# Layer 0's self attention in a two-layer decoder: the output projection written to another PSUM bank, the residual's moments taken later

## The reference

```python
x = _layernorm(x + _L0_attn_ref(x, Wg, bg, Wv, bv, Wo, bo))
g = x @ Wg.T + bg;  v = x @ Wv.T + bv            # then split into heads
dot = einsum('bhid,bhjd->bhij', g, g)
corr = dot / (nrm[..., :, None] * nrm[..., None, :] + 1e-08)
corr = (corr * m + 1.0) / 2.0                    # m: causal mask
denom = mean(corr, axis=3) + 0.5
sum_inv = sum(1.0 / denom, axis=2, keepdims=True)    # over the rows
weighted = corr * (1.0 / (denom * sum_inv))[..., None]
attn = softmax(weighted * m + (1.0 - m) * NEG)
out = einsum('bhij,bhjd->bhid', attn, v)  ->  out @ Wo.T + bo
```

## Time and profile before

| | us |
|---|---|
| median of 3 runs | 2441.64 |
| lowest, highest run | 2436.2, 2446.11 |
| profiled execution, own time | 2436.9 |
| its span in the trace | 2435.0 |
| PE busy | 2222.8 (91%) |
| DVE busy | 1337.9 (55%) |
| ACT busy | 1107.0 (45%) |
| POOL busy | 917.7 (38%) |

### The profile page before, as it was taken

The page is one execution under the profiler, slowest core; times in us unless marked ns, Lnnn a source line. Parts: engine busy times, 40 slices in busy tenths (PEclk is TensorE's granted clock), DMA queues, the critical chain, the costliest instruction groups (busy, mean ns, idle before and its releaser), DMA issues. The chain is left out here.

```text
span 2435.0 us, 44061 instructions
## 1 busy us (share of the span) xinstructions
PE 2222.8 (91%) x16870; PEld 1746.6 (72%) x16870; DVE 1337.9 (55%) x2486; ACT 1107.0 (45%) x1904; POOL 917.7 (38%) x935
## 2 busy tenths in 40 slices
PE   6888886899997999999999799999995999999993
PEld 5777775566665666757777588888884888888893
DVE  6888886688885870024555468888784111111113
ACT  3677775456655664434333355555552111111113
POOL 4777774244444680000110234544453122222221
PEclk8999998899999999999999899999997999999997
DMA  4444553101011679460220323333332766566665
GB/s 144 112 113 116 159 138 90 57 18 53 28 62 43 237 253 301 144 217 5 66 70 27 122 79 103 107 105 105 107 120 103 272 185 196 180 176 189 191 203 149
DMA packets 204607, 313.05 MB, mean 129 GB/s; under 512 B 63601, under 2 KB 183153, under 8 KB 191089
## 3 DMA queue, kind: packets, MB, share of 16 engines
q1 hardware_dynamic: 184336, 255.12, 33.2%
q0 software_dynamic: 13440, 17.90, 4.1%
q10 hardware_dynamic: 6624, 37.23, 3.9%
HBM read 188.75 MB, written 121.45 MB: 127 GB/s over the span
## 5 line engine op out<-in xcount | busy, mean ns | idle before, releaser
L2758 ACT ACTIVATE dec_area<-me_ps_h 128x512 f32<-128x512 f32 (+1 forms) x160 | 88.7, 555 | 423.5 <-PE me_ps_h L2736 414.8
L2799 DVE TENSOR_SCALAR me_yo<-me_ps_y,moe_xg 128x256 f32<-128x256 f32 x72 | 34.8, 484 | 429.6 <-PE me_ps_y L2746 410.6
L2674 POOL DMA_INDIRECT xo<-me_yo,me_row x72 | 112.8, 1566 | 410.4 <-DVE me_yo L2799 347.1
L2209 POOL TENSOR_TENSOR l1x_e<-l1x_e,l1x_ri 128x1024 f32<-128x1024 f32 x64 | 121.8, 1903 | 240.3 <-DVE l1x_ri L2469 240.3
L2736 PE MATMUL me_ps_h<-me_xt,me_w 128*128 128x256 f32 (+1 forms) x1056 | 210.0, 357 | 0.0
L2746 PE MATMUL me_ps_y<-me_w,dec_area 128*128 128x256 f32 x944 | 209.2, 379 | 0.7 <-DVE me_yo L2799 0.7
L2746 PEld LDWEIGHTS me_ps_y<-me_w,dec_area 128*128 128x128 f32 x944 | 178.7, 190 | 25.1 <-issue 1.1
L2736 PEld LDWEIGHTS me_ps_h<-me_xt,me_w 128*128 128x128 f32 x1056 | 181.7, 190 | 20.2
L892 POOL TENSOR_TENSOR l0x_e<-l0x_e,l0x_ri 128x1024 f32<-128x1024 f32 x64 | 120.1, 1897 | 187.8 <-DVE l0x_ri L1112 187.8
L2308 PE MATMUL l1x_ps_p<-l1x_xct,dec_area 128*128 128x256 f32 x512 | 126.1, 392 | 0.8 <-ACT l1x_xct L2394 0.7
L2346 PE MATMUL l1x_ps_o<-dec_area,l1x_ot 128*128 128x256 f32 x512 | 120.4, 389 | 1.4 <-ACT l1x_ot L2417 1.4
(11 more groups left out here) (414 smaller groups left out, 5334.8 us busy)
## 6 DMA issues: line engine op xcount, KB each, us to landing
me_w<-in_w SPq DMA_DIRECT2D x33, 2048.0 KB, 9.5
xs<-dec_zero SPq DMA_DIRECT2D x31, 1032.0 KB, 6.9
k<-kv_kt ACTq DMA_DIRECT2D x16, 1024.0 KB, 4.6
v<-kv_va ACTq DMA_DIRECT2D x16, 1024.0 KB, 4.7
l1x_kt<-k SPq DMA_DIRECT2D x16, 1024.0 KB, 5.1
l1x_va<-v SPq DMA_DIRECT2D x16, 1024.0 KB
moe_w_first<-in_w SPq DMA_DIRECT2D x7, 2048.0 KB, 9.5
moe_xg<-xs SPq DMA_DIRECT2D x32, 258.0 KB, 2.9
```

What stands on the lines that cost most here:

```text
L2209: pool.tensor_tensor(e[:, n % 2, u, :, :], e[:, n % 2, u, :, :], spread(ri[:, n % 2, u, :], P), ALU.mult).then_inc(e_scaled, 1)
L2674: pool.indirect_dma_start(token_rows, bass.IndirectOffsetOnAxis(row[:, j % 2, q:q + 1], 0), yo[:, j % 2, q, :], None, compute_op=ALU.add). ...
L2758: act.activation(h[:, j % 2, 2 * i:2 * i + 2, 0:P * size(j)], ps_h[i % HB][:, :, 0:P * size(j)], ACT.Gelu).then_inc(gelued, 1)
```

## The change

The output projection of a tile is written to `ps_a[0]`, in columns 16 to 79 of each of its four parts of 128, instead of 256 adjacent columns of `ps_e[1]`. `residual` reads it there. The transposes of set j = 1 no longer wait for `residual_done`, nor the projection for the copies `et_copied`. Instead `sum_inverse` of tile n waits for the residual of tile n-2, and the denominators of tile n wait for the projection of tile n-2. On VectorE the two moment operations leave `residual` and become a step of their own, behind the even weighting of the next round. On TensorE the second set of transposes is placed ahead of the value projection, and the third ahead of the sum of inverses. ScalarE copies the value projection between the second and the third set instead of behind all four.

```diff
@@ -571,6 +571,9 @@
 
                     return ps_a[0][:, i, 0:H]
 
+                def parts(a):
+                    return a.rearrange("p (a b) -> p a b", a=4)
+
                 def correlate(n, u):
                     i = 2 * n + u
                     item_done(dve, tanh_done, i)
@@ -591,6 +594,8 @@
                     item_done(dve, rows_summed, n)
                     if n + 1 < TILES:
                         dve.wait_ge(ops_copied, 2 * (n + 1) + 1)
+                    if n >= 2:
+                        item_done(dve, multiplied, n - 2)
                     dve.tensor_scalar(small(1), flat(st[:, n % 2, 0, :, :]), 0.25 / S, 1.0, ALU.mult, ALU.add).then_inc(denom_done, 1)
                     item_done(dve, denom_done, n)
                     slot_free(dve, inv_summed, n, 2)
@@ -619,15 +624,18 @@
                     item_done(dve, multiplied, n)
                     item_done(dve, x_biased, n)
                     slot_free(dve, normed, n, 2 * G)
-                    dve.tensor_tensor(r[:, g % 2, t, :], ps_e[1][:, 0:2, :].rearrange("p a b -> p (a b)"), xb[:, n % 2, :],
+                    dve.tensor_tensor(parts(r[:, g % 2, t, :]), ps_a[0][:, :, H:H + D // 4], parts(xb[:, n % 2, :]),
                                       ALU.add).then_inc(residual_done, 1)
+
+                def moments(n):
+                    g, t = n // G, n % G
                     item_done(dve, residual_done, n)
                     slot_free(dve, mv_done, n, 2)
                     dve.bn_stats(stats[:, n % 2, :], r[:, g % 2, t, :]).then_inc(stats_done, 1)
                     item_done(dve, stats_done, n)
                     slot_free(dve, ln_done, g, 2)
                     dve.bn_aggr(mv[:, g % 2, t, :], stats[:, n % 2, :]).then_inc(mv_done, 1)
-                walk([(1, weigh_even), (0, lambda n: fold_bias() if n == 0 else None), (0, lambda n: correlate(n, 1)), (2, divide), (0, row_sums), (2, residual), (-1, lambda n: correlate(n, 0)), (0, fitness)])
+                walk([(1, weigh_even), (0, lambda n: fold_bias() if n == 0 else None), (3, moments), (0, lambda n: correlate(n, 1)), (2, divide), (0, row_sums), (2, residual), (-1, lambda n: correlate(n, 0)), (0, fitness)])
 
             @block.tensor
             def _(pe):
@@ -681,6 +689,8 @@
 
                 def sum_inverse(n):
                     item_done(pe, inv_done, n)
+                    if n >= 2:
+                        item_done(pe, residual_done, n - 2)
                     if n + 1 < TILES:
                         pe.wait_ge(ops_copied, 2 * (n + 1) + 1)
                     pe.matmul(ps_a[0][:, 0, 0:H], ones[:, :], flat(st[:, n % 2, 1, :, :]), start=True, stop=True).then_inc(inv_summed, 1)
@@ -692,8 +702,6 @@
                         slot_free(pe, divided, n, 1)
                     elif j == 1 and n == 0:
                         pe.wait_ge(bo_done, 1)
-                    elif j == 1:
-                        slot_free(pe, residual_done, n, 1)
                     else:
                         pe.wait_ge(et_copied, i - 1)
                     for h in range(4):
@@ -724,12 +732,11 @@
                     if n == 0:
                         pe.wait_ge(w_loaded, 64)
                     item_done(pe, divided, n)
-                    item_done(pe, et_copied, n, 4)
                     for k in range(2):
-                        last = pe.matmul(ps_e[1][:, 0:2, :].rearrange("p a b -> p (a b)"), ot[:, n % 2, k, :], w_o[:, k, :],
+                        last = pe.matmul(ps_a[0][:, :, H:H + D // 4], ot[:, n % 2, k, :], w_o[:, k, :].rearrange("p (a b) -> p a b", a=4),
                                          start=k == 0, stop=k == 1)
                     last.then_inc(multiplied, 1)
-                walk([(3, multiply), (2, lambda n: transpose_e(n, 0)), (0, project_v), (2, lambda n: transpose_e(n, 1)), (1, sum_inverse), (2, lambda n: transpose_e(n, 2)), (2, lambda n: transpose_e(n, 3)), (0, lambda n: score(n, 1)), (2, apply), (-1, transposes), (-1, lambda n: score(n, 0))])
+                walk([(3, multiply), (2, lambda n: transpose_e(n, 0)), (2, lambda n: transpose_e(n, 1)), (0, project_v), (2, lambda n: transpose_e(n, 2)), (1, sum_inverse), (2, lambda n: transpose_e(n, 3)), (0, lambda n: score(n, 1)), (2, apply), (-1, transposes), (-1, lambda n: score(n, 0))])
 
             @block.scalar
             def _(act):
@@ -766,9 +773,9 @@
                     slot_free(act, e_transposed, i, 4, 2)
                     act.activation(e[:, n % 2, u, :, :], wt[:, u, :, :], ACT.Exp).then_inc(exped, 1)
 
-                def copy_et(n):
+                def copy_et(n, which):
                     slot_free(act, applied, n, 1)
-                    for j in range(4):
+                    for j in which:
                         item_done(act, e_transposed, 4 * n + j)
                         act.activation(et[:, j // 2, 4 * (j % 2):4 * (j % 2) + 4, :], ps_e[j % 2][:, :, :], ACT.Copy).then_inc(et_copied, 1)
 
@@ -778,7 +785,7 @@
                     slot_free(act, stored[t], g, 1, 16)
                     act.activation(y[:, t, :], r[:, g % 2, t, :], ACT.Identity, scale=lnm[:, g % 2, 0, t:t + 1],
                                    bias=lnm[:, g % 2, 1, t:t + 1]).then_inc(normed, 1)
-                walk([(8, normalise), (2, lambda n: exponentials(n, 1)), (0, lambda n: guard(n, 0)), (2, copy_et), (0, copy_v), (0, lambda n: guard(n, 1)), (1, lambda n: exponentials(n, 0)), (-1, copy_ops)])
+                walk([(8, normalise), (2, lambda n: exponentials(n, 1)), (0, lambda n: guard(n, 0)), (2, lambda n: copy_et(n, (0, 1))), (0, copy_v), (2, lambda n: copy_et(n, (2, 3))), (0, lambda n: guard(n, 1)), (1, lambda n: exponentials(n, 0)), (-1, copy_ops)])
         kit.clear_semaphores()
 
 
```

## The result

The changed kernel takes 2417.95 us, the median of four runs (2411.71 to 2419.68), beside 2440.53 for the kernel before (2436.2 to 2446.11). The ratio is 0.9901 with a 95% interval of 0.9889 to 0.9913: 22.6 us less, where 24.9 was forecast. The time is 1.2 us above the forecast one, closer than the gain is, because the forecast started from 2441.6 and the kernel before came out at 2440.53 with one more run. The profiled execution took 2417.48 us.

What follows compares the result with a forecast made beforehand. The prediction took a 10.73 us chain of dependent steps across engines, with neither VectorE nor TensorE full, to bound the head loop. Saving 0.86 in 29 rounds gave 2441.6 - 24.9 = 2416.7 us, range 2408 to 2433.

Steps and rivals of the forecast that it cites:

- The ring: Layer 0 self-attention head loop: chain of dependent steps across engines that sets one round, forecast from 10.73 to 9.87 us.
- the two rings: Scores wait for transposes held by the residual, and for the even correlation; removing only the first wait buys 0.19 us.
- The independent pair: VectorE: even correlation does not need the residual's result, so starts 0.08 us before its recorded end, at 234.50.
- TensorE in time: TensorE's reordered work before the scores ends at 235.50, against their release at 235.83: 0.33 us to spare.
- The added waits: Sum of inverses waiting for residual, denominator for projection: cost nothing, at most 0.03 us a round (1 us).
- The short pieces: Projection in four 64-column pieces: forecast free; rival 0.80 us more a tile, gain only 11.3 us, 2430, chance 0.09.
- Where the moments go: VectorE, behind the even weighting: moments fit before the odd correlation with 0.26 us to spare.
- The rival of slower moments: Moments double to 1.12 us beside GpSimd's multiplication; gain 0.56 a round, 16.2 us, 2425; chance 0.11.
- The sum: Whole loop: 29 rounds times 0.86 us gives 24.9 us less.
- The rival of starved issue: TensorE starved of instructions: ten stalls of 3.80 us cost 38 against 24.9 gained, 2455; chance 0.06.
- Prologue and tail: Stretches where one tile alone runs through the engines: forecast no change.

Runs made afterwards that it cites:

- the two halves: Changed kernel with moments left directly behind the residual: 2432.25 us, 0.9962 of before; kernel before with only the moments moved: 2437.18 us, 0.999 of before.
- the old order: Changed kernel with TensorE's and ScalarE's orders put back as in the kernel before: 2425.76 us, 0.9928 of before.
- the doubled operation: Changed kernel with the first moment operation issued twice, first into an unread spare tile: 2414.87 us, 0.9895 of before.

## Why the prediction was right, point by point

**The ring.** Right to 0.01: 9.88 against 9.87. The even correlation starts 2.97 after the row sums (forecast 2.98), the scores 4.32 (4.31), the odd correlation 6.61 (6.61). That both halves are needed, which the two rings implied, is shown by the two halves run alone.

**The independent pair.** Residual and correlation start 0.28 apart (226.41 to 226.69), as the rows had it; the reading of the Trainium skill ("Advanced Engine Details and Errata", "The Read-Write Bubble") as a fixed cost after every instruction, which would have cost 3.2 us, does not hold here.

**TensorE in time.** Right. It was computed to have 0.33 to spare. The last set starts at 227.14 and would have let the scores start 0.56 later, at 227.70; they start at 228.04, so it has 0.34. The printed idle time of 0.27 counts from the recorded end of the set.

**The added waits.** Cost nothing in undisturbed rounds. The sum of inverses starts 3.28 after the row sums, as computed (234.80 - 231.52); only with the old order does it meet the residual.

**The short pieces.** Nothing: 0.97 against 0.96, and VectorE's residual 0.36 both times. The rival is out.

**Where the moments go.** 0.42 and 0.18 in the new place beside GpSimd's multiplication, 0.43 and 0.18 before. The rival of slower moments is out. The room of 0.26 was borne out by the doubled operation to within 0.04.

**The sum.** 29 x 0.85 = 24.6 came about in the rounds. The step that was mis-sized is the assumption that the waits for issue stay what they were. The mean of the traces beyond the undisturbed rounds is 8.2 us before and 11.0 changed, 2.8 more, which leaves 21.8 of loop; the medians say 22.6. That the sum is off by so little is in part luck. Outside the last round the time beyond the undisturbed rounds grew by 7.4 us in the mean, from 3.6 to 11.0, and the 4.7 us that the last round lost before went away; the prediction reckoned with neither. The rival of starved issue was thus real in kind, at a fifth of its price of 38 us outside the last round and less than a tenth in the sum. Its evidence was read too narrowly: full DMA engines at the time of the wait are not its mark, since three waits of the changed kernel fell where these engines were nearly idle, each of them right behind a burst.

**Prologue and tail.** Left at nothing. From the last row sums to the next stage it took 30.1 and 30.2 us in the two traces of before, and 28.4 (380.57 to 409.00), 29.0 and 30.0 in the three of the changed kernel. So the tail gave 0.1 to 1.8 us that were not in the sum.

## What to carry to other kernels

When a wait is removed, look for what would have been last without it, and how far away it is; here it was 0.19 us, and only shortening both chains together gave 0.85 a round. Write the ring of one round as a sum of start-to-start distances and check that it gives the measured period before changing a term. Read the room on an engine from start to start too, and cut large background transfers into spaced pieces, because they can hold up the transfers that bring an engine its instructions without being in any chain of waits.

## What was not expected of the hardware

An engine's waits for issue, up to 2.6 us each in this loop (3.80 and 5.15 in the last round of before), go with the bursts of an unrelated store and end 2.4 to 2.9 us after a 16 KB instruction packet has started: 1 MB once a round goes with 7 to 14 us over the loop (18 with the orders of before), the same 1 MB in four spaced pieces with 1.4, and no such store with 0.5 to 1.5. And VectorE's second, independent moment operation costs 0.34 from start to start where its recorded duration is 0.42.
